# Sums of the softmax taken from the accumulator output of the exponentials, in the last six layers of an AdaLN kernel

## The reference

```python
def attn_layer(x, Wqkv, qs, ksc, Wo):            # 16 heads of 64, windows of 32 tokens
    q, k, v = jnp.split(x @ Wqkv, 3, -1)
    q = l2norm(q) * qs; k = l2norm(k) * ksc      # then rotated, with a scale by position
    out = local_attention(q, k, v)
    return out @ Wo

def local_attention(q, k, v):                    # each window sees itself and the one before
    sim = jnp.einsum('bhwie,bhwje->bhwij', bq, bk2) * QK_SCALE
    sim = jnp.where(mask, -jnp.finfo(sim.dtype).max, sim)
    attn = jax.nn.softmax(sim, -1)
    return jnp.einsum('bhwij,bhwje->bhwie', attn, bv2)

for i in range(DEPTH):                           # DEPTH = 6
    x = attn_layer(shift_tokens(x), ...) + x
    x = ffn_layer(shift_tokens(x), ...) + x      # layer norm, two products, gelu, product
```

## Time and profile before

| | |
|---|---|
| median of 3 runs | 2546.63 us (2536.71 to 2547.93) |
| the profiled execution | 2536.73 us, its span 2535.0 us |
| busy share of the span | PE 92%, PEld 66%, DVE 79%, ACT 73%, POOL 50% |
| the windowed layers | from about 765 us to the end; a round every 69.7 us |
| mean granted clock of TensorE | 0.965 |

### The profile page before, as it was taken

The page is one execution under the profiler, slowest core; times in us unless marked ns, Lnnn a source line. Parts: engine busy times, 40 slices in busy tenths (PEclk is TensorE's granted clock), DMA queues, the critical chain, the costliest instruction groups (busy, mean ns, idle before and its releaser), DMA issues.

```text
span 2535.0 us, 60549 instructions
## 1 busy us (share of the span) xinstructions
PE 2325.2 (92%) x22196; PEld 1663.6 (66%) x22196; DVE 2004.9 (79%) x4390; ACT 1850.2 (73%) x4176; POOL 1277.4 (50%) x1093
## 2 busy tenths in 40 slices
PE   6798689999966899999999999999999999999996
PEld 3476368888754666666666666666667666666762
DVE  2599477777777888888888898888888888888862
ACT  2255478888744788877888888887788788878772
POOL 0132010000005877776777777776777677766650
PEclk8899799999987999999999999999999999999997
DMA  2000112221002111012111111102111111111110
GB/s 86 9 2 1 44 69 75 75 75 67 27 22 77 35 30 38 25 39 56 41 39 33 52 41 27 39 25 56 41 39 39 50 35 33 27 51 44 25 29 21
DMA packets 37812, 103.90 MB, mean 41 GB/s; under 512 B 7953, under 2 KB 13393, under 8 KB 34705
## 3 DMA queue, kind: packets, MB, share of 16 engines
q1 hardware_dynamic: 37520, 100.04, 13.8%
HBM read 50.61 MB, written 2.23 MB: 21 GB/s over the span
## 4 chain that ended last, share of the span: by engine, by line
PE 40%; DVE 16%; ACT 4%; issue 3%; DMA 3%; POOL 3%; SPq 1%; DVEq 0%; ACTq 0%; POOLq 0%
PE w_psP L1766 12%; PE w_psO L1816 6%; PE w_psF L1713 4%; PE w_psA L1799 4%; PE w_psF L1734 4%; PE w_psT L1773 3%; PE w_psS L1789 3%; DVE w_rs L67 2%; DVE w_bb L1915 2%; DVE w_ab L1914 2%; DVE w_sm L1937 2%; PE w_psF L1738 2%; PE w_psS L1783 1%; DVE w_mx L1931 1%; DVE w_nrm L1921 1%
## 5 line engine op out<-in xcount | busy, mean ns | idle before, releaser
L2006 POOL TENSOR_TENSOR w_ab<-w_ab,w_bb 128x512 f32<-128x512 f32 x384 | 491.9, 1284 | 210.5 <-DVE w_bb L1915 210.4
L2011 POOL TENSOR_TENSOR w_ab<-w_ab,w_nrm 128x512 f32<-128x512 f32 x384 | 397.7, 1052 | 125.1 <-DVE w_nrm L67 125.1
L1866 ACT ACTIVATE w_pb<-w_psS,w_mx 128x96 f32<-128x96 f32 x1536 | 391.2, 360 | 3.3 <-DVE w_mx L1931 2.6
L1842 ACT ACTIVATE w_sq<-w_psP 128x512 f32<-128x512 f32 x384 | 232.0, 604 | 157.5 <-PE w_psP L1766 152.1
L2016 POOL TENSOR_TENSOR w_pb<-w_pb,w_sm 128x768 f32<-128x768 f32 x192 | 282.4, 1471 | 111.6 <-DVE w_sm L1938 111.6
L1766 PE MATMUL w_psP<-w_hi,w_xh 128*128 128x512 f32 x576 | 300.6, 522 | 24.8 <-DVE w_bb L1915 12.2
L1914 DVE TENSOR_TENSOR w_ab<-w_psP,w_tabs 128x512 f32<-128x512 f32 x384 | 263.1, 685 | 63.9 <-ACT w_sq L1842 56.9
L1931 DVE TENSOR_REDUCE w_mx<-w_psS 128x4 f32<-128x384 f32 x384 | 201.7, 547 | 115.5 <-PE w_psS L1789 115.5
L1873 ACT ACTIVATE w_pT<-w_psA 128x512 f32<-128x512 f32 (+1 forms) x384 | 233.0, 607 | 64.0 <-PE w_psA L1799 63.2
L1921 DVE TENSOR_REDUCE w_nrm<-w_sq 128x8 f32<-128x512 f32 x384 | 258.7, 674 | 5.9 <-ACT w_sq L1842 3.8
L1915 DVE TENSOR_TENSOR w_bb<-w_psP,w_tabs 128x512 f32<-128x512 f32 x384 | 261.3, 681 | 0.0
(11 more groups left out here) (300 smaller groups left out, 5094.8 us busy)
## 6 DMA issues: line engine op xcount, KB each, us to landing
e_gb<-gate_rows SPq DMA_DIRECT2D x16, 1024.0 KB, 4.7
X<-tables_layer SPq DMA_DIRECT2D x48, 256.0 KB, 3.5
X<-w_v SPq DMA_DIRECT2D x48, 256.0 KB, 3.1
e_raw<-in_w_moe SPq DMA_DIRECT2D x32, 256.0 KB, 5.2
w_raw<-in_w_qkv SPq DMA_DIRECT2D x20, 384.0 KB, 3.7
X<-tables_layer SPq DMA_DIRECT2D x48, 128.0 KB, 3.1
w_o<-in_w_o SPq DMA_DIRECT2D x6, 512.0 KB, 4.6
w_xs<-H SPq DMA_DIRECT2D x24, 128.0 KB, 2.2
```

What stands on the lines that cost most here:

```text
L1866: last = act.activation(pb[k % 2][:, 4 * j + q, WIN * (k % 2):], psS[j][:, q * KEYS:(q + 1) * KEYS], ACT.Exp, bias=mx[:, 4 * j + q:4 * j + ...
L2006: pool.tensor_tensor(a, a, bb[:, i % 2, :], ALU.add).then_inc(s["ad"], 1)
L2011: pool.tensor_tensor(a, a, nrm[k // 2][:, 1, 8 * (i % 8):8 * (i % 8) + 8].unsqueeze(2).to_broadcast([128, 8, DH]), ALU.mult).then_inc(s["n ...
```

## The change

The exponentials of `Xe` get an accumulator output: each also writes the sum of its 96 results to its column of `sm`. `Xd` loses the sum over `pb` and the semaphore wait between it and the reciprocal, and keeps the two waits ahead of it. `ORDER` stays, as do all buffers.

```diff
@@ Xe
                     for q in range(4):
                         last = act.activation(pb[k % 2][:, 4 * j + q, WIN * (k % 2):], psS[j][:, q * KEYS:(q + 1) * KEYS],
-                                              ACT.Exp, bias=mx[:, 4 * j + q:4 * j + q + 1])
+                                              ACT.Exp, bias=mx[:, 4 * j + q:4 * j + q + 1], accum_out=sm[k % 2][:, 4 * j + q:4 * j + q + 1])
                     last.then_inc(s["e"], 1)
@@ Xd
-                    ch = Chain(dve, s_sum, 1, r * NBLK + k)
                     dve.wait_ge(s["e"], r * UA + 2 * k + 2)
                     wait(dve, s["pn"], r * NBLK + k - 1)
-                    ch.link(dve.tensor_reduce(sm[k % 2][:, :], pb[k % 2][:, :, WIN * (k % 2):], AX_X, ALU.add))
                     dve.reciprocal(sm[k % 2][:, :], sm[k % 2][:, :]).then_inc(s["r"], 1)
```

## The result

The changed kernel takes 2592.39 us (median of 4 runs, 2589.97 to 2598.53) against 2545.25 before (median of 4): a ratio of 1.0202, 95% interval 1.018 to 1.0224, which is 51 us (46 to 57) on 2545; the medians are 47 apart. The two profiled executions are 53.3 us apart (spans 2588.3 and 2535.0).

What follows compares the result with a forecast made beforehand. TensorE was taken to set the pace, busy 68.11 of 69.72 us a round. Seven late starts sum to 2.37 us a round, times 24 rounds 57 us; on the median 2546.63 that forecasts 2603, range 2557 to 2665.

Steps and rivals of the forecast that it cites:

- the 10 us added for the median of before: Profiled execution 2536.73 us would give 2594; the median of three runs, 2546.63, lies 10 higher, giving 2603.
- The price of a read: On ScalarE, each accumulator read delays the next exponential by 0.10 us: 0.40 a group, 6.4 a round.
- both bounds: Limits on a read's price on ScalarE: 0 if it vanishes in the overlap, 0.33 us if behind a finished exponential.
- rival 1: The read on ScalarE costs more, 0.136 us each: 3.77 us a round, +90 us, 2637; chance 16 in 100.
- The places: Seven TensorE starts delayed by ScalarE: `S0.0` 0.09, `T1.1` 0.22, `S2.0` 0.28, `P0.1` 0.64, `At3.1` 0.32, `S6.0` 0.41, `T0.2` 0.41.
- The reads of blocks 0 and 3, said to be free: Exponential groups `Xe0` and `Xe3` end in ScalarE's gaps or before the wait at `back`, adding no TensorE delay.
- `P0.1`: TensorE start needing the bank `Ve3.1` empties: margin 0.16 us, lateness 0.80, so 0.64 us later each round.
- what `Xe3.0` does to `At2.0` is taken up by the 1.46 us in front of `back`: Lateness from block 3's first exponentials is absorbed by TensorE's 1.46 us wait for the tail's normalised tokens; 0 added.
- The premise under "removed": Dropping VectorE's sums, 7.6 us a round, moves the tail's norm by 0.14 us at most; no gain taken.
- Rival 4: VectorE paces mid-round; without its sums the 1.46 us wait before `back` goes, 35 us faster, 2512; chance 6 in 100.
- The times 24: All 24 rounds, the last ones included, were each counted as losing 2.37 us, 57 us in all.

Runs made afterwards that it cites:

- no_sums: Kernel before without VectorE's sums and without accumulator outputs; reciprocals are taken of a constant. Ratio 0.9989 to before, -3 us.
- reads_1_2: Changed kernel with accumulator outputs for blocks 1 and 2 of each round only, VectorE's sums for the others. Ratio 1.0157 to before, +40 us.

## Why the prediction was right

- **Sign and size.** The mechanism holds: ScalarE's lateness reaches TensorE at single places of the written order. 53 us between the profiled executions, 57 forecast; 2592 for 2603. The medians of the two kernels are 47 apart, as the 10 us added for the median of before shrank to 9 there and to 2 after.
- **The price of a read.** 0.10 forecast, 0.09 to 0.10 measured; both bounds and the 0.136 of rival 1 fall. The overlap of about 93 ns that the Trainium skill (ScalarE: Activation LUTs, "What ACT_TABLE_LOAD costs") states fits neither pair here: exponentials out of PSUM start 224 ns apart, and a pair with its read 317 ns. The measurement decides.
- **The places.** Seven named, seven found, six of them within 0.14 us of their forecast. The reads of blocks 0 and 3, said to be free, are free.
- **The step that failed inside the sum.** `P0.1` was put at 0.64. Its start is 0.55 later, but 0.29 of that is no loss: its first matmul then lasts 0.50 instead of 0.79, and the next starts that much sooner. And "what `Xe3.0` does to `At2.0` is taken up by the 1.46 us in front of `back`" took that wait for slack. It is not: from `Sq0.0` to `back` runs a chain of ScalarE (two groups of exponentials, `Te`, `Ve`, `xh`), GpSimd (from `xl` on) and the norm, and both groups' lateness, 2 x 0.37 = 0.74, comes out between `P0.1` and `back`: 0.26 + 0.48, against 0.64 + 0 in the sum. That the two errors nearly cancel is luck as far as the reasoning goes, though both count the same two groups.
- **The premise under "removed".** The sums were said to be able to move the norm by 0.14 us at most, because its first product starts 0.14 behind ScalarE. The result (nothing) is right. But in these two kernels the wait before `back` does not hang on that start: the changed kernel's norm begins 0.48 earlier behind `xh` and ends no earlier.
- **Rival 4** (VectorE paces the middle) falls by no_sums: -3 us and the wait still there, for -35. The wait is VectorE's by name only. In a round the sums were removed where nothing waited for them.
- **The times 24.** The 22 rounds between the second `xh` and the last are 2.0 us longer on average, not 2.2, since rounds at a layer's end lose less. The end loses more. The windows from the last `xh` to the end, before and then after:

```profile
2303.26:2535.00 231.74, 200.40 (x2160) 131.39 (x2158) 149.89 (x323) 149.96 (x356) 112.06 (x92) 0.92 0.11 26
```

```profile
2346.76:2588.30 241.54, 206.62 (x2158) 134.33 (x2157) 130.35 (x300) 162.77 (x524) 112.01 (x92) 0.90 0.10 25
```

  That is 9.8 us more, as much as four rounds pay; I had counted it like the rest. That ScalarE has ever less of other engines' work to hide behind there is my reading, and no run shows it by itself. How much of it is the lower clock (0.90 for 0.92) stays open.

## What to carry to other kernels

Price an added instruction by the distance of starts around one like it, then follow it through the engine's written order: it costs where the engine has no wait of its own before the next consumer, and nothing where it has, however busy the engine is on average. Work taken off an engine pays only where a wait ends with it. A wait before a matmul is slack only if its chain does not pass the engine that you slow; check from which start it keeps a constant distance.

## What the hardware showed unexpectedly

- VectorE instructions of 128 x 4 that read and write SBUF last 0.16 us where GpSimd's work is cut to 8 columns (light_pool), and typically 0.97 beside its full `tensor_tensor`, ending with it. Keeping GpSimd out of the later ones was worth 35 us.
- A wait of TensorE of 1.5 to 1.7 us before `back` was followed, in some rounds and not in others, by 3 to 7 us at a granted clock of 0.5, which cost 1.5 to 3 us each. Behind 1.71 us it was most frequent (seven rounds of reads_1_2), but no_sums has six behind 1.49 and the kernel before none behind 1.46. What decides between rounds with the same wait is open.
